# Row maxima of attention scores, taken bank by bank instead of for both banks at once

## The reference, cut to what matters

```python
h = layernorm(x) * (1 + ca) + sa              # x: 16 batches, 1024 tokens, 256 features
q = (h @ Wq.T).reshape(b, t, 8, 64)
kv = h @ Wkv_down.T                           # rank 64
k = (kv @ Wk_up.T).reshape(b, t, 8, 64)
v = (kv @ Wv_up.T).reshape(b, t, 8, 64)
scores = einsum('bqhd,bkhd->bhqk', q, k) * 64 ** -0.5
attn = softmax(scores, axis=-1)               # needs the maximum of each row of 1024 keys
x = x + ga * (einsum('bhqk,bkhd->bqhd', attn, v).reshape(b, t, 512) @ Wo.T)
h = layernorm(x) * (1 + cb) + sb
x = x + gb * (h @ weight.T + pooled(h) @ disha)
```

## Time and profile before

| | before |
|---|---|
| median of 3 runs | 3562.01 us (3559.07 to 3562.82) |
| the profiled execution | 3557.84 us |
| its span, first to last instruction | 3555.9 us |
| PE busy | 3328.4 us, 94% |
| POOL busy | 2510.2 us, 71% |
| DVE busy | 2463.9 us, 69% |
| ACT busy | 1672.1 us, 47% |
| largest group of DVE | L972, 1016 reduces, 1240.8 us |

### The profile page before, as it was taken

The page is one execution under the profiler, slowest core; times in us unless marked ns, Lnnn a source line. Parts: engine busy times, 40 slices in busy tenths (PEclk is TensorE's granted clock), DMA queues, the critical chain, the costliest instruction groups (busy, mean ns, idle before and its releaser), DMA issues.

```text
span 3555.9 us, 50728 instructions
## 1 busy us (share of the span) xinstructions
PE 3328.4 (94%) x14886; PEld 1920.0 (54%) x14886; DVE 2463.9 (69%) x2846; ACT 1672.1 (47%) x3075; POOL 2510.2 (71%) x1513
## 2 busy tenths in 40 slices
PE   5899999989999999999999999999999989999996
PEld 3444555545555564555646555464555645556454
DVE  4667767677676766767777676775767767676663
ACT  1444545444454444545444454544545445454443
POOL 1667677767776677667777677777777776777775
PEclk7999999999999999999999999999999999999998
DMA  1001010010101001010010100101010010100101
GB/s 56 30 24 51 22 59 20 28 49 30 52 19 62 21 25 51 28 55 19 31 50 22 60 20 28 48 31 52 19 62 19 28 53 24 54 25 28 36 30 33
DMA packets 98083, 129.34 MB, mean 36 GB/s; under 512 B 11121, under 2 KB 62449, under 8 KB 97777
## 3 DMA queue, kind: packets, MB, share of 16 engines
q1 hardware_dynamic: 97776, 125.64, 10.2%
HBM read 41.11 MB, written 16.81 MB: 16 GB/s over the span
## 4 chain that ended last, share of the span: by engine, by line
PE 74%; DVE 9%; issue 8%; POOL 6%; ACT 3%; DMA 0%; POOLq 0%; ACTq 0%; DVEq 0%; SPq 0%
PE ps_mix L544 22%; PE ps_max L587 12%; PE ps_score L565 12%; PE ps_score L567 10%; PE ps_side_b L532 5%; PE ps_side_b L649 5%; DVE neg_max L972 4%; POOL prob_sum L833 3%; PE ps_side_a L636 3%; PE ps_side_b L667 3%; DVE recip L952 2%; POOL x_in L852 1%; POOL rstd L819 1%; DVE h_lo L994 1%; ACT h_whole L772 1%
## 5 line engine op out<-in xcount | busy, mean ns | idle before, releaser
L833 POOL TENSOR_TENSOR prob_sum<-prob_sum,probs 128x1024 f32<-128x1024 f32 x768 | 1837.7, 2393 | 436.5 <-ACT probs L732 387.5
L972 DVE TENSOR_REDUCE neg_max<-ps_max 128x1 f32<-128x1024 f32 x1016 | 1240.8, 1221 | 694.4 <-PE ps_max L587 690.5
L732 ACT ACTIVATE probs<-ps_score 128x512 f32<-128x512 f32 x2048 | 1114.4, 597 | 1260.8 <-PE ps_score L567 1249.7
L544 PE MATMUL ps_mix<-probs,values 128*64 128x512 f32 x4096 | 994.6, 606 | 0.0
L565 PE MATMUL ps_score<-query,key_hi 128*128 128x512 f32 x2048 | 887.5, 433 | 46.6 <-issue 30.2
L567 PE MATMUL ps_score<-query_m,key_lo 128*128 128x512 f32 x2048 | 813.3, 397 | 0.0
L587 PE MATMUL ps_max<-key_hi,query 128*128 128x512 f32 x2032 | 669.7, 411 | 65.9 <-DVE neg_max L972 65.7
L565 PEld LDWEIGHTS ps_score<-query,key_hi 128*128 128x128 f32 x2048 | 387.6, 189 | 545.3 <-issue 409.9
L833 POOL TENSOR_TENSOR prob_sum<-probs 128x1024 f32<-128x1024 f32 x128 | 303.4, 2370 | 506.4 <-ACT probs L732 506.3
L544 PEld LDWEIGHTS ps_mix<-probs,values 128*64 128x64 f32 x4096 | 249.2, 136 | 481.1 <-issue 481.1
L952 DVE RECIPROCAL recip<-recip 128x128 f32<-128x128 f32 x512 | 481.5, 942 | 27.3 <-ACT recip L783 27.3
(11 more groups left out here) (115 smaller groups left out, 2725.8 us busy)
## 6 DMA issues: line engine op xcount, KB each, us to landing
query_m<-query SPq DMA_DIRECT2D x128, 512.0 KB, 3.2
x_in<-in_L_attn_x_dram SPq DMA_DIRECT2D x16, 1024.0 KB, 6.0
x_mid<-in_L_attn_x_dram SPq DMA_DIRECT2D x64, 256.0 KB, 7.0
out_dram<-x_mid SPq DMA_DIRECT2D x64, 256.0 KB, 2.2
h_t<-gates_scratch SPq DMA_DIRECT2D x16, 256.0 KB, 6.6
query_m<-max_row SPq DMA_DIRECT2D x128, 4.0 KB
mixed<-in_L_wmod_dram SPq DMA_DIRECT2D x1, 1536.0 KB, 10.3
mixed<-in_L_attn_Wq_dram SPq DMA_DIRECT2D x1, 512.0 KB, 4.9
```

The costliest lines, as they stand in the source:

```text
L544: last = nc.tensor.matmul(ps_mix[g % 2][j * R:j * R + R, :], values[par][:, k, :], probs[:, s % RING, j * HALF:(j + 1) * HALF], start=(k = ...
L732: nc.scalar.activation(probs[:, s % RING, half * HALF:(half + 1) * HALF], ps_score[half], ACT.Exp, scale=SCALE).then_inc(exps_done, 1)
L833: nc.gpsimd.tensor_tensor(out=total[:, :], in0=before, in1=probs[:, s % RING, :], op=ALU.add).then_inc(adds_done, 1)
L972: nc.vector.tensor_reduce(neg_max[:, m:m + 1], z.max_bank(m, ps_max, ps_scores)[:, :], AX_X, ALU.max, negate=True).then_inc(maxima_done, 1)
```

## The change

The two banks of an item are reduced one after the other, each into its own column of a new tile `neg_half` (2 x 64 columns), and each reduce increments `maxima_done`. So this semaphore counts two for each item, and its other counts are doubled. Each of TensorE's two matmuls now increments `max_scores_ready`, so the first reduce may start after the first matmul. Each of them also waits by itself: the first for the first bank's reduce of the item before, the second for the second bank's. At the last item of each group of eight, VectorE waits for its own reduces and takes the elementwise minimum of the two halves (128x8 numbers, the maxima are negated) into `neg_max`, and increments a new semaphore `maxima_joined`, for which `max_row` waits instead of `maxima_done`. The matmuls, their operands and the steps of all pieces stay as they are.

```diff
+        neg_half = sb("neg_half", [P, 2, STEPS])
...
+        maxima_joined = sem("maxima_joined")
...
-                            pe.wait_ge(maxima_done, STEPS - MAX_LAG)
+                            pe.wait_ge(maxima_done, 2 * (STEPS - MAX_LAG))
...
-                    need(pe, maxima_done, STEPS * b + m - (0 if z.has_c else 1))
                     bank = z.max_bank(m, ps_max, ps_scores)
                     for half in range(2):
-                        last = nc.tensor.matmul(bank[:, half * HALF:(half + 1) * HALF],
+
+                        need(pe, maxima_done, 2 * (STEPS * b + m - (0 if z.has_c else 1)) + half - 1)
+                        nc.tensor.matmul(bank[:, half * HALF:(half + 1) * HALF],
                                                 query[:, hm, qt * P:(qt + 1) * P],
                                                 key_hi[kpar][:, half * HALF:(half + 1) * HALF],
-                                                start=True, stop=True)
-                    last.then_inc(max_scores_ready, 1)
+                                                start=True, stop=True).then_inc(max_scores_ready, 1)
...
-                        need(pe, maxima_done, STEPS * b + NT * (i + 1))
+                        need(pe, maxima_joined, GROUPS * b + i + 1)
...
-                        need(dve, max_scores_ready, STEPS * b + m + 1)
-                        nc.vector.tensor_reduce(neg_max[:, m:m + 1], z.max_bank(m, ps_max, ps_scores)[:, :], AX_X, ALU.max, negate=True).then_inc(maxima_done, 1)
+                        for half in range(2):
+                            need(dve, max_scores_ready, 2 * (STEPS * b + m) + half + 1)
+                            nc.vector.tensor_reduce(neg_half[:, half, m:m + 1],
+                                                    z.max_bank(m, ps_max, ps_scores)[:, half * HALF:(half + 1) * HALF],
+                                                    AX_X, ALU.max, negate=True).then_inc(maxima_done, 1)
+                        if m % NT == NT - 1:
+
+                            group = slice(m + 1 - NT, m + 1)
+                            need(dve, maxima_done, 2 * (STEPS * b + m + 1))
+                            nc.vector.tensor_tensor(neg_max[:, group], neg_half[:, 0, group], neg_half[:, 1, group],
+                                                    ALU.min).then_inc(maxima_joined, 1)
```

## The result

The changed kernel takes **3604.38** (median of 4 runs, 3603.70 to 3605.47), the kernel before 3560.54 in the runs beside them: ratio 1.0125, 95% interval 1.0108 to 1.0143. It is **44 slower**, where 27 faster was forecast. All times are in us. First the cores' view, then lines of the page's parts 1, 4 and 5, then waits over the whole span (total us, times, longest us). They answer to the earlier trace rows.

The account below looks back on a forecast made before the run. TensorE was taken as the bound, busy 94% of the span and stalled by VectorE's reduces. Fourteen batches of 1.42 us gave 20, the first 5, the last 3, lead-in -1: 27 less, 3535 for the median, range 3503 to 3560.

Parts of the forecast that it names:

- The minimum: VectorE's 128x8 minimum per group of eight items: 0.24 to 0.28 us, bounds 0.15 and 0.45, 128 times.
- The pair of reduces: Two half reduces on VectorE take 1.35 us together (bounds 1.22 and 1.40), 0.13 more than the whole one.
- The long stall: TensorE waiting for VectorE's reduce in odd steps without side work between the pairs of matmuls: gain 0.33 us each.
- the short one: TensorE's stall where a transpose lies between the pairs of matmuls, as in steps 30 and 31: gain 0.21 us.
- The second wait on TensorE: The added wait of the maxima matmuls, when already fulfilled: costs 0, upper bound 0.02 us.
- The gains of steps 5, 7 and 9: Three long stalls a batch, 1.0 us, counted as lost because TensorE waits in step 11 behind GpSimd's unbroken stretch.
- Steps 23, 31, 39, 47 and 29: Four short stalls gain 0.84 us a batch, the long one of step 29 gains 0.33.
- Steps 55 and 57: VectorE has no idle time there, so pair and minimum make the stretch 0.15 us longer per batch.
- Steps 63 and 1: Stalls around the batch's end: 0.33 us for step 63, some 0.15 for step 1, 0.48 shorter together.
- The forecast's slower case: A large fixed part makes a half reduce 0.86 us or longer, every wait lengthens: about 3607, chance 0.09.
- Nothing comes of it: Rival: VectorE's 165 us of added work, delaying the end of every group, takes the gain: 3555 to 3569, chance 0.17.
- All of it stays: Rival: the stretch of steps 5 to 17 moves too, 3.5 us a batch: 3500, chance 0.13.

Follow-up runs that it names:

- e1_one_input: The changed kernel with the minimum taken by a reduce over one tensor instead of an elementwise minimum of two: 3521.52, ratio 0.9903 to the kernel before.
- pair of shifted kernels: Kernel before and e1_one_input, each with GpSimd's second normalization half at step 8 instead of 10, its statistics at steps 6 and 7: 3544.22 and 3491.37.

## Why the prediction was wrong

**The step that failed** is "*The minimum.*" in the part on the change, a term of the sum: 0.24 to 0.28 of VectorE, with bounds 0.15 and 0.45. It was 1.57 on average and 2.2 at most, five times the upper bound. The price came from a row of nearly the same size, the aggregate of 0.18, but that has one input. What counted was the form: two inputs in SBUF. The bound could have been read from the kernel before. It has such operations, and the view of a line shows it (the same three durations, ns):

```profile
L994 DVE TENSOR_TENSOR h_lo<-h_whole,h_hi x64: 672/1224/2640, 36.3 to 3150.8; 128x512 fp32r<-128x512 f32 x64
```

The same 128x512 operation takes 0.67 once and 2.64 another time. By its records, the 19 that start beside no GpSimd instruction take 0.67 to 0.69; the 45 that start during one all end 0.55 after it has ended. So the spread of 2.0 on one shape is a wait inside the operation, and it was there to be bounded: the minimum could take from 0.17 to about 2.4, the length of an add. L1002, 0.83 in the earlier trace rows, was read there without asking what made it longer than the 0.69 of the same shape with one input in PSUM; 60 of its 64 end 0.55 behind a GpSimd instruction in the same way.

**What followed from it.** "Nobody waits for it" was right, and "it delays what is queued behind it" too, with the places: step 57 and step 1. With a minimum of 2.10, the estimate's own scheme makes step 57 longer by 1.93 than with the 0.17 of e1_one_input, less 0.18 since L1013 takes 0.68 here and 0.86 there: 1.75. In the seven batches without a fall of the clock there, step 57 of the changed kernel is 1.75 longer than that of e1_one_input (+1.81 against +0.06). In the other seven it is 2.6 to 3.4 longer. This second effect, the fall of the clock, stood in none of the cases. The six other minima of a batch cost little (steps 12 to 20 lose 0.3 more than in e1_one_input, the others nothing), though those of steps 23 to 47 take 2.1 as well; the likely reason, not tested, is that VectorE has idle time behind them; in the first and the last batch, which have other work, more of them cost something.

**The rest of the sum held**, as e1_one_input shows, which is the change with the minimum that was priced:

- The pair of reduces: forecast 1.35, measured 1.29. The long stall gains 0.40 instead of 0.33, the short one 0.22 instead of 0.21. The page that the prediction quoted from the Trainium skill ("VectorE: DVE Perf Modes", section "The DRAIN you can't avoid") says that a fulfilled wait between two operations costs nothing extra, and the prediction's sum by it was 1.30 for the pair. By that rule, the trace agrees: the second reduce starts 0.08 before the first has ended, as operations without a wait do in the earlier trace rows. The 0.05 that the prediction set for the wait was not there.
- The second wait on TensorE costs nothing: with both waits, the long stalls become shorter by all that the two releases can give.
- The gains of steps 5, 7 and 9 were lost again in step 11: -1.20 and +1.24. ScalarE's wait for GpSimd (75.6 in 16 before, 94.1 in e1) grew by 1.2 each, where 1 was forecast, and PE's waits show it too (total us, times, longest us; first two lines before, then e1). The pair of shifted kernels confirmed it.

```profile
ACT h_hi L772 <- POOL mod L859: 75.6, 16, 13.1
...
PE ps_side_a L636 <- ACT h_whole L772: 11.9, 15, 0.8
```

```profile
PE ps_side_a L638 <- ACT h_whole L774: 30.4, 15, 2.1
```

- Steps 23, 31, 39, 47 and 29: -1.27, forecast -1.17.
- Steps 55 and 57: forecast 0.15 longer, measured 0.16 shorter in e1, since the minimum is 0.17 there and the pair shorter.
- Steps 63 and 1: forecast 0.48 shorter, measured 0.10. In the batches that end without the loop's branch, step 63 is 0.40 shorter; in those that end with it, it is 0.3 to 1.7 longer. The view of waits puts this down to issue: 30.2 in 6 waits of L565 before, 39.2 in 6 of L567 in e1. It wasn't tried what makes the branch cost more.
- Per batch 1.34 against 1.42, fourteen 19 against 20; the first batch 6.8 against 5. The last gave 11.8 instead of 3, of which 4.4 stand in step 19 alone. Lead-in: 0 instead of -1.

So the sum of 27 less stands near the measured 36 less once the minimum costs what it was priced at. In part that nearness is luck: within a batch, 0.38 too much at steps 63 and 1 was made up by 0.31 too little at 55 and 57, and most of the 9 between the sums comes from the last batch. Range and chances were drawn around that price and missed the sign.

**The rivals.** The forecast's slower case, 3607, has the right size and sign and the wrong mechanism: it needed a half reduce of 0.86, which took 0.68. "Nothing comes of it" had the right engine, a delay at the ends of groups, and priced it at 0.36. "All of it stays" fell with step 11.

**What stays open.** How the 83 divide between waiting and the clock. The time at 0.50 is 252 in the changed kernel and 184 in e1; work at half the clock takes twice as long, so the 68 cost at most 34, an estimate. At step 57 alone, the seven batches with a fall are together 9.3 longer, against e1_one_input, than seven without one. No run kept the standstills and took the fall of the clock away.

## What to carry to other kernels

Price an added operation by its form (which inputs, in which memory), and look at the smallest and largest duration of such operations, not at the mean of one of similar size: a wide spread on one shape can be a wait that the view of waits doesn't show, as it was here. A small operation put into a full queue costs what it may have to wait for, so here a reduce over one tensor in the place of a minimum of two made 83 of difference. And where one engine ran without a pause and another waited for its end, time won ahead of that end was lost there; moving part of the stretch let some 17 of it through.

## What the runs showed of the hardware

- A VectorE operation of 8 columns with two SBUF inputs took 0.17 alone and up to 2.24 while GpSimd worked; 100 of 128 ended 0.02 to 0.03 after GpSimd's add had ended. Longer operations are held as well: of 512 columns, L994 took 0.67 to 2.64 in the kernel before, of 1024 columns, L987 took 1.22 once and up to 3.33 in the changed one. The view of waits shows nothing of it: it counts as busy time. The one-input form took 0.17 beside the same adds.
- Halving GpSimd's adds costs little: two of 1.30 instead of one of 2.40, 154 for 896 adds, and was worth 62 as long as something waited for them.
- The granted clock fell to 0.50 for 3.4 after TensorE had stood idle 1.88, not at each such place: in 7 of 14 at step 57. At step 1 it fell in 8 of 14, after 1.36 to 1.48; in the kernel before at neither. In steps 11 to 13, where TensorE's standstill is 1.2 longer in e1_one_input than before, it falls in all 14 batches of the loop; in the kernel before in one. So a wait of TensorE can cost more than its own length: the eight matmuls of `ps_mix` behind it took 3.42 instead of 1.94. Time at 0.50 in e1 is 44 above before, although e1 is faster.
